# A decoder layer with routed experts on one core: zero rows by DMA, logits behind the first maxima, and a head group's last value products among the next group's first scores

## The chip, the core and the metric

The kernel runs on one core of a Trainium2 chip. TensorE (PE) multiplies matrices into PSUM, VectorE (DVE), ScalarE (ACT) and GpSimd (POOL) work on rows, and SyncE (SP) issues most of the DMAs. The metric is the time of one execution on the device in microseconds (us), the median of several runs.

## The reference, cut to what matters

```python
# x (4, 1024, 256), 16 heads of 16, rotary part of 32; cross attention over 77 keys; 8 experts, two for each token
x = layernorm(x + attention(x))        # causal, scores = (q.k + q_rope.k_rope) / sqrt(48), then W_o
x = layernorm(x + cross_attention(x, ctx, mask))   # softmax(q.k / 16) @ v, masked
probs = softmax(x @ Wr.T)              # the logits of the router
topw, topi = top_k(probs, 2); topw /= sum(topw)
y = sum over the two experts of gate * (silu(x @ w1[e]) * (x @ w3[e])) @ w2[e]
return layernorm(x + y)
```

## The kernel before, in words

Everything is in one program with a hand-written order on each engine and semaphores between them. After a start-up (constants, zeroed rows, projections of batch 0) it runs four batches, and after them the expert part over 72 blocks. Batch 0 and batch 3 are written out; batches 1 and 2 are one loop that runs twice.

**Attention of a batch** is done in four groups of four heads (`HG`). For each group there are two passes over scores. The first, `s1_unit` on PE (lines 754 and 758) and `maxima` on DVE (1271, 1274), only finds the row maxima; 24 units and one transposition (762) end in a 16 KB DMA of `nmaxT` into row 127 of `qs` (`MROW`, line 651). The second pass, `s2_unit` (777, 778), has the maximum folded in through that row, 12 steps of four heads, each followed on ACT by an exponential into `pT` (1142). On eight of the twelve steps, the diagonal ones, the last among them, POOL then zeroes later keys (`zero_later_keys`, 472). `pv_step` (792) multiplies with the values one step later (`LAG` = 1), and after the last step of a group ACT copies the result out of PSUM (`oT`, 1150). The units of the next group's first pass are strewn among this group's second pass by `due`, from `FIRST` and the tables of column counts; `ALONE_AT`, `COUNT_AT` and `PAIRED_AT` do this for group 0, in which the routing of the batch before also still runs.

**Operands.** `qs` and `kas` hold for two sets the rows 0 to 31 (parts of q or k), 32 to 95 (rotary parts) and 127; the rows 96 to 126 (`KROWS` to `MROW`, 31 rows) must be zero since the products run over 127 or 128 rows. `kbs` is the same for the low part of k. `kas` set 0 is used as other storage (`xTh`, `xTl`) for the projections of the next batch, and `kbs` for the cross attention, so their zero rows are written anew in each batch, by POOL: `zero_keys` (449) once the projections are through, and line 533 when the cross attention is through. Rows 96 to 126 of `qs` set 0 are zeroed once and stay zero.

**SP's order** (`first_groups`, 608, for the next batch): rotary rows of `qs` (592), `save_part` 0 to 5 (602), rotary rows of `kas`, the row of ones (606), `save_part` 6 and 7, a wait until all parts are in DRAM, loads of q and k of group 0 (570), then set 1, then, when the cross attention is through (642), the rotary rows of `kbs` and the low part of k (583). Later transfers on this queue, `nmaxT` too, stand behind these.

**Between two attentions** PE transposes `oT` (941), `att` (949), multiplies with W_o (732), transposes x for the cross attention (970), computes its scores (982), transposes its probabilities (992), multiplies with the values (999), transposes again (970) and computes the logits (1009, 32 products of 8 columns). `fill` puts the first maxima of the next batch's group 0 between these. On DVE `keep` and `neg` (1307, 1308) come first, then the chain of the normalizations (1335), and when all maxima are done `choose` (1413 on) does the routing; ACT gives it one exponential (1181), today before the exponentials of the next attention. POOL scatters the routed rows (`SENT`, 485) in groups 0 and 1 of the next attention.

Of the kernel before, what the change touches and what calls it, by code (L numbers as in the profile page):

```python
# [18 lines left out]
F32 = mybir.dt.float32  # L19
# [5 lines left out]
ACT = mybir.ActivationFunctionType  # L25
# [3 lines left out]
B, T, D = 4, 1024, 256  # L29
NT = T // P  # L30
# [4 lines left out]
NG = NH // HG  # L35
# [6 lines left out]
MROW = P - 1  # L42
# [37 lines left out]
LAG = 1  # L80
# [3 lines left out]
ALONE = SECOND  # L84
ALONE_AT = (0, 1, 3, 5, 7, 10, 12, 14)
AHEAD = 1
COUNT_AT, PAIRED_AT = 9, 15
LATE = (43, 39, 39, 39)
FIRST, SPARE = 1, 11
SENT = ((0, 0, 0, 2, 2, 2, 2, 2), (2, 2, 2, 0, 0, 0, 0, 0))  # L90

# [13 lines left out]
def layer(nc, x, ctxT, mask, w_all, kwT, qw, vwT, qb, kb, vb, wrT, w1, w3, w2, ident, causal, before,  # L105
          numbers, filling, rope, out):
    ctx = ExitStack()
    with ctx:
# [121 lines left out]
        with nc.Block() as block:  # L230
# [25 lines left out]
            @block.gpsimd  # L256
            def _(pool):
                pool.dma_start(xa[:, :, :], x[0].rearrange("(t p) d -> p t d", p=P)).then_inc(s_x, 16)

                pool.dma_start(xs[E * CAP:ROWS], filling[E * P:]).then_inc(s_sc, 16)  # L260
                pool.memset(wr[:, :, :], 0.0).then_inc(s_init, 1)
                pool.memset(m_all[:, :, :, :], 0.0).then_inc(s_init, 1)
                pool.memset(vall[:, :, :], 0.0).then_inc(s_init, 1)
                pool.memset(vaug[:, :, :, HD:HD + 1], 1.0).then_inc(s_init, 1)
                pool.memset(px[:, :, :], 0.0).then_inc(s_init, 1)
                pool.memset(one[:, :], 1.0).then_inc(s_init, 1)
                pool.memset(taken[:, :], 0.0).then_inc(s_init, 1)
                pool.memset(nhalf[:, :], -0.5).then_inc(s_init, 1)
                pool.wait_ge(s_init, 8)
                pool.memset(kbs[KROWS:MROW, :, :].bitcast(F32), 0.0).then_inc(s_zl, 1)  # L270
                pool.wait_ge(s_zl, 1)
                pool.memset(qs[KROWS:MROW, 0, :, :].bitcast(F32), 0.0).then_inc(s_zero, 1)
                pool.wait_ge(s_zero, 1)
                pool.memset(kas[KROWS:MROW, 1, :, :].bitcast(F32), 0.0).then_inc(s_zero, 1)
                pool.wait_ge(s_zero, 2)
# [144 lines left out]
        with nc.Block() as block:  # L420
            @block.gpsimd
            def _(pool):
# [19 lines left out]

                def zero_keys(b):

                    pool.wait_ge(s_pr, b * N_PROJ + QK[3] + 1)
                    pool.sem_inc(s_seen, 1)
                    pool.wait_ge(s_rs, b * 4 + 4)
                    pool.sem_inc(s_seen, 1)
                    pool.memset(kas[KROWS:MROW, 0, :, :].bitcast(F32), 0.0).then_inc(s_zk, 1)
                    pool.wait_ge(s_zk, b + 1)  # L450
                    pool.sem_inc(s_seen, 1)

                for m in range(4):
                    rope_add(0, m)
                    rope_low(0, m)
                zero_keys(0)
                for s in s_stg:
# [31 lines left out]
                def batch(b, then, ahead):  # L489
# [23 lines left out]

                    if then:
                        pool.wait_ge(s_tri, (b + 1) * NG * len(DIAG))
                        pool.sem_inc(s_seen, 1)
                        zero_keys(b + 1)
                    power(0, 0, s_ve1, s_pow1)
# [8 lines left out]
                    power(1, 1, s_ve2, s_pow2)  # L527
                    if then:
                        pool.wait_ge(s_t7, (b + 1) * NT)
                        pool.sem_inc(s_seen, 1)  # L530
                        pool.wait_ge(s_pow2, (b + 1) * 2)
                        pool.sem_inc(s_seen, 1)
                        pool.memset(kbs[KROWS:MROW, :, :].bitcast(F32), 0.0).then_inc(s_zl, 1)
                        pool.wait_ge(s_zl, b + 2)
                        pool.sem_inc(s_seen, 1)

# [27 lines left out]
            def _(sp):  # L564
# [43 lines left out]
                def first_groups(b, first):  # L608
# [8 lines left out]
                    place_rope(kas[:, 0], 2, s_qk[0])  # L617
                    place_ones(0)
                    for m in range(6, 8):
                        save_part(b, m)  # L620
# [19 lines left out]
                    if not first:  # L640
                        sp.wait_ge(s_t7, b * NT)
                        sp.sem_inc(s_spw, 1)
                    place_rope(kbs, 3, s_kb)
                    for h in range(2):
                        load_klow(b, 0, h)
# [82 lines left out]
            def _(pe):  # L728
# [119 lines left out]
                def first_maxima(b, n):  # L848

                    if n == 0:  # L850

                        pe.wait_ge(s_zk, b + 1)
                        if isinstance(b, int) and b == 0:
                            pe.wait_ge(s_zero, 1)
                        pe.wait_ge(s_vc, b * 4 + 4)
                        if not isinstance(b, int) or b > 0:
                            pe.wait_ge(s_t3r, b * NT)
                        heads_here(b, 0, 0)
                    if n == SECOND:
                        heads_here(b, 0, 1)  # L860
                    s1_unit(b, 0, n)
# [7 lines left out]
                def attention(b, then, ahead):  # L869
# [15 lines left out]
                    for g in range(NG):  # L885
                        done = 0
                        if g == 0:
                            pe.wait_ge(s_zl, b + 1)
                            heads_here(b, 1, 0)
# [7 lines left out]
                        for u in range(N_PV):  # L897
# [20 lines left out]
                            if u >= LAG:  # L918
                                pv_step(b, g, u - LAG)
                        for u in range(N_PV - LAG, N_PV):  # L920
                            pv_step(b, g, u)
                        assert g + 1 == NG or done == N_S1

                def batch(b, then, ahead):
# [78 lines left out]
                    turn(x2, s_ln2, s_t8, s_t8r)  # L1003
                    fill(12, 13, 14)
                    for hf in range(2):
# [5 lines left out]
                        ins.then_inc(s_t9, 1)  # L1011
                    fill(*range(15, N_S1))

# [91 lines left out]
            def _(act):  # L1105
# [25 lines left out]

                def batch(b, then):
                    for g in range(NG):
                        for u, (j, c) in enumerate(S2_STEPS):
# [4 lines left out]
                            for h in range(HG):  # L1139
                                n = g * N_S2 + u * HG + h  # L1140
                                act.wait_ge(s_s2, b * NG * N_S2 + n + 1)
                                act.activation(pT[:, u % 2, h, 0:q1 - q0], ps[:, s2_bank(n), q0 - w0:q1 - w0], ACT.Exp,  # L1142
                                               scale=ATT_SCALE).then_inc(s_exp, 1)
                            if then and g == NG - 1:
                                for m in LAST_ACT[u]:
                                    proj(b + 1, m)
                        act.wait_ge(s_pv, (b * NG + g + 1) * N_PV)
                        if g == 1:
                            act.wait_ge(s_left, b + 1)
                        act.activation(oT[:, g, :], ps[:, 6:8, :].rearrange("p c n -> p (c n)"), ACT.Copy).then_inc(s_oT, 1)  # L1150
                    for t in range(NT):
# [27 lines left out]
                    act.activation(x2b[:, :, 0:D], x2[:, :, 0:D], ACT.Copy).then_inc(s_x2b, 1)  # L1179
                    act.wait_ge(s_le, b + 1)  # L1180
                    act.activation(lg[:, 1, :, :], lg[:, 0, :, :], ACT.Exp).then_inc(s_lex, 1)

                for u in range(N_PROJ):
                    proj(0, u, True)
                batch(0, True)
                with act.Fori(1, B - 1) as b:
                    batch(b, True)
                batch(B - 1, False)

# [473 lines left out]
```

## Time and profile before

| | us |
|---|---|
| median of 3 runs | 1621.0 |
| lowest and highest | 1615.82 and 1627.38 |
| the profiled execution | 1616.89 |
| its span in the profile | 1615.2 |
| start-up, up to the first scores of batch 0 | 103.7 |
| PE busy | 1371.1 (85%) |
| DVE, ACT, POOL busy | 790.3, 624.1, 359.3 |

A profile gives for each engine the instructions with their start, and in brackets how long the engine was idle before one and what ended that idle time. The span is the time from the first to the last instruction.

### The profile page before, as it was taken

How to read it: one execution, taken by the hardware profiler on the slowest of the kernel's cores; microseconds unless marked ns; L12 is line 12 of the kernel's file. 1: busy time of each engine (PE TensorE's matmuls, PEld its weight loads, DVE VectorE, ACT ScalarE, POOL GpSimd, SP SyncE). 2: the span in 40 equal slices, each digit the busy share in tenths (PEclk: the TensorE clock that was granted, in tenths of full speed). 3: DMA queues.
4: the chain of work that ended last, by engine and by line, in shares of the span. 5: the costliest groups of instructions: out<-in, count | busy, mean ns of one | idle time of the engine just before them, and what ended most of it. 6: DMA issues, size and time to landing. Idle time of an engine off the chain costs nothing.

```text
span 1615.2 us, 25041 instructions
## 1 busy us (share of the span) xinstructions
PE 1371.1 (85%) x7580; PEld 959.9 (59%) x7581; DVE 790.3 (49%) x1636; ACT 624.1 (39%) x1327; POOL 359.3 (22%) x434
## 2 busy tenths in 40 slices
PE   3688999879899976989988799997359999999980
PEld 2545566655555564655566556555248888888870
DVE  3364452677544386644348655506733333333325
ACT  2124556313455521445642244562423333333324
POOL 5201112210411401131230132110332222222225
PEclk9789999968999996999988699998579999999995
DMA  4752113830321382032156212217311111111119
GB/s 148 205 97 41 29 20 100 199 63 1 87 47 42 118 171 41 12 83 40 43 165 123 40 46 47 40 42 260 105 56 53 49 49 52 52 49 49 52 38 310
DMA packets 87836, 131.80 MB, mean 82 GB/s; under 512 B 14944, under 2 KB 46944, under 8 KB 87584
## 3 DMA queue, kind: packets, MB, share of 16 engines
q1 hardware_dynamic: 74064, 100.98, 26.0%
q0 software_dynamic: 7936, 24.20, 4.6%
q10 hardware_dynamic: 5744, 5.43, 1.1%
q8 instruction: 53, 0.87, 0.2%
q14 instruction: 39, 0.32, 0.1%
HBM read 70.34 MB, written 40.98 MB: 69 GB/s over the span
## 4 chain that ended last, share of the span: by engine, by line
PE 70%; DVE 9%; issue 6%; DMA 6%; POOL 4%; ACT 2%; SPq 2%; ACTq 0%; POOLq 0%; DVEq 0%
PE ps L1089 13%; PE ps L777 11%; PE ps L754 10%; PE ps L778 8%; PE ps L1076 8%; PE ps L792 8%; DMA kas<-scr_k 3%; PE ps L732 3%; PE ps L758 2%; PE ps L1097 2%; DVE nmax L1274 2%; POOL xs L485 1%; PE ps L1059 1%; PE ps L1009 1%; DVE x L1335 1%
## 5 line engine op out<-in xcount | busy, mean ns | idle before, releaser
L1142 ACT ACTIVATE pT<-ps 128x512 f32<-128x512 f32 (+3 forms) x768 | 344.5, 493 | 349.0 <-PE ps L778 348.9
L1274 DVE TENSOR_REDUCE nmax<-ps 128x1 f32<-128x640 f32 (+3 forms) x256 | 258.5, 1024 | 118.6 <-PE ps L758 113.8
L777 PE MATMUL ps<-qs,kas 128*128 128x512 f32 (+2 forms) x768 | 308.7, 410 | 8.9 <-DMA qs<-nmaxT 5.3
L754 PE MATMUL ps<-kas,qs 127*128 127x512 f32 (+2 forms) x768 | 247.8, 412 | 27.1 <-DMA kas<-scr_k 16.2
L778 PE MATMUL ps<-qs,kbs 127*128 127x512 f32 (+2 forms) x768 | 268.0, 357 | 0.0
L777 PEld LDWEIGHTS ps<-qs,kas 128*128 128x128 f32 x768 | 150.2, 196 | 140.8 <-ACT pT L1142 102.2
L472 POOL TENSOR_SCALAR_AFFINE_SELECT pT<-pT 128x512 f32<-128x512 f32 x128 | 81.2, 634 | 661.9 <-ACT pT L1142 661.8
L754 PEld LDWEIGHTS ps<-kas,qs 127*128 127x128 f32 x768 | 152.0, 220 | 62.2 <-issue 12.9
L1271 DVE TENSOR_REDUCE nmax<-ps 128x2 f32<-128x256 f32 (+3 forms) x128 | 104.4, 825 | 151.0 <-PE ps L758 150.1
L792 PE MATMUL ps<-pT,vaug 128*17 128x512 f32 (+3 forms) x1536 | 161.2, 491 | 15.7 <-POOL pT L472 15.6
L778 PEld LDWEIGHTS ps<-qs,kbs 127*128 127x128 f32 x768 | 149.9, 195 | 5.4
L1076 PE MATMUL ps<-w2s,hidT 128*128 x576 | 136.1, 379 | 0.8 <-ACT hidT L1219 0.8
L1089 PE MATMUL ps<-w13h,xbh 128*128 x288 | 120.1, 417 | 0.1
L1076 PEld LDWEIGHTS ps<-w2s,hidT 128*128 128x128 f32 x576 | 109.1, 190 | 18.2 <-issue 1.0
L1219 ACT ACTIVATE hidT<-ps 128x512 f32<-128x512 f32 x72 | 43.0, 598 | 188.8 <-PE ps L1097 188.8
L1569 DVE TENSOR_TENSOR hid<-ps,sil 128x512 f32<-128x512 f32 x72 | 49.8, 692 | 134.1 <-PE ps L1089 134.1
L1089 PE MATMUL ps<-w13h,xbl 128*128 x288 | 114.6, 398 | 0.0
L1089 PE MATMUL ps<-w13l,xbh 128*128 x288 | 112.9, 392 | 0.0
L758 PE MATMUL ps<-cst_b 128*128 128x128 bf16 x512 | 105.8, 250 | 0.0
L758 PEld LDWEIGHTS ps<-cst_b 128*128 128x128 bf16 x512 | 44.2, 109 | 80.5 <-issue 75.9
L426 POOL TENSOR_TENSOR mark<-nhalf 128x1 f32<-128x1 f32 x76 | 14.0, 184 | 291.6 <-DVE yb L1579 271.8
L550 POOL DMA_INDIRECT sums<-yb,ib x72 | 70.8, 984 | 32.6 <-issue 32.3
(199 smaller groups left out, 1775.3 us busy)
## 6 DMA issues: line engine op xcount, KB each, us to landing
xb<-xs SPq DMA_DIRECT2D x72, 129.0 KB, 2.1
qs<-rs SPq DMA_DIRECT2D x32, 256.0 KB, 6.1
scr_q<-stg SPq DMA_DIRECT2D x16, 512.0 KB, 2.7
scr_k<-stg SPq DMA_DIRECT2D x16, 512.0 KB, 3.6
kas<-rs SPq DMA_DIRECT2D x32, 256.0 KB, 6.2
qs<-scr_q SPq DMA_DIRECT2D x64, 128.0 KB, 5.4
kas<-scr_k SPq DMA_DIRECT2D x64, 128.0 KB, 6.2
kbs<-scr_k SPq DMA_DIRECT2D x64, 128.0 KB, 4.1
```

The source lines that it names most:

```text
L472: pool.affine_select(pT[:, u % 2, :, 0:P], pT[:, u % 2, :, 0:P], pattern=[[0, HG], [1, P]], compare_op=ALU.is_ge, fill=zero, base=0, chann ...
L550: pool.indirect_dma_start(out=sums[:, :], out_offset=bass.IndirectOffsetOnAxis(ib[:, d, :], 0), in_=yb[:, d, :], in_offset=None).then_inc( ...
L754: ins = pe.matmul(ps[:, slot + bank, 0:n_k], qs[0:MROW, g % 2, h, i * P:(i + 1) * P], kas[0:MROW, g % 2, h, k0:k0 + n_k], start=True, stop ...
L758: ins = pe.matmul(ps[:, slot + own, i * P - k0:k1 - k0], idb, mask_q, start=False, stop=True)
L777: pe.matmul(o, kas[:, g % 2, h, j * P:(j + 1) * P], qs[:, g % 2, h, w0:q1], start=True, stop=False)
L778: pe.matmul(o, kbs[0:MROW, h, j * P:(j + 1) * P], qs[0:MROW, g % 2, h, w0:q1], start=False, stop=True).then_inc(s_s2, 1)
L792: ins = pe.matmul(ps[h * 32:h * 32 + HD + 1, 6 + c, q0 - c * HALF:HALF], vaug[:, j, g * HG + h, :], pT[:, u % 2, h, 0:q1 - q0], start=j == ...
L1076: ins = pe.matmul(ps[:, 7, 0:D], hidT[:, p, c, :], wide(w2s, e, c), start=c == 0, stop=c == F // P - 1)
L1089: ins = pe.matmul(ps[:, bank + p, :], a[:, p, c, :], wide(w, e, part, c), start=k == 0, stop=k == len(terms) - 1)
L1142: act.activation(pT[:, u % 2, h, 0:q1 - q0], ps[:, s2_bank(n), q0 - w0:q1 - w0], ACT.Exp, scale=ATT_SCALE).then_inc(s_exp, 1)
L1271: dve.tensor_reduce(nmax[:, k:k + NT + 1:NT], ps[:, slot:slot + 2, 0:(i + 1) * P], AX.X, ALU.max, negate=True).then_inc(s_s1r, 1)
L1274: dve.tensor_reduce(nmax[:, k:k + 1], ps[:, slot:slot + 2, :].rearrange("p s n -> p (s n)")[:, 0:(i + 1) * P], AX.X, ALU.max, negate=True) ...
```

## The change

Four things are done. The 31 zero rows of `kas` set 0 and of `kbs` come by a DMA on SP's queue from the rows of `qs` that stay zero, and POOL's memsets go, the one at the start too. The logits stand behind all first maxima, and their exponential on ACT behind the first four exponentials of the next attention. A group's last value products run behind the first four scores of the next group, with the copy of `oT` behind those four exponentials. The tables that place the units and POOL's scatters are set anew.

```diff
-ALONE_AT = (0, 1, 3, 5, 7, 10, 12, 14)
+ALONE_AT = (0, 5, 6, 8, 10, 13, 15, 17)
-COUNT_AT, PAIRED_AT = 9, 15
+COUNT_AT, PAIRED_AT = 12, 18
-FIRST, SPARE = 1, 11
-SENT = ((0, 0, 0, 2, 2, 2, 2, 2), (2, 2, 2, 0, 0, 0, 0, 0))
+FIRST, SPARE = 6, 11
+SENT = ((0, 0, 0, 4, 0, 0, 0, 0), (3, 3, 3, 3, 0, 0, 0, 0))
...
-                pool.memset(kbs[KROWS:MROW, :, :].bitcast(F32), 0.0).then_inc(s_zl, 1)
-                pool.wait_ge(s_zl, 1)
...
-                def zero_keys(b):
-
-                    pool.wait_ge(s_pr, b * N_PROJ + QK[3] + 1)
-                    pool.sem_inc(s_seen, 1)
-                    pool.wait_ge(s_rs, b * 4 + 4)
-                    pool.sem_inc(s_seen, 1)
-                    pool.memset(kas[KROWS:MROW, 0, :, :].bitcast(F32), 0.0).then_inc(s_zk, 1)
...
-                        pool.memset(kbs[KROWS:MROW, :, :].bitcast(F32), 0.0).then_inc(s_zl, 1)
...
                     place_rope(kas[:, 0], 2, s_qk[0])
                     place_ones(0)
+                    if first:
+                        sp.wait_ge(s_zero, 1)
+                    sp.dma_start(kas[KROWS:MROW, 0, :, :].bitcast(F32), qs[KROWS:MROW, 0, :, :].bitcast(F32)).then_inc(s_zk, 16)
                     for m in range(6, 8):
                         save_part(b, m)
...
                     place_rope(kbs, 3, s_kb)
+                    sp.dma_start(kbs[KROWS:MROW, :, :].bitcast(F32), qs[KROWS:MROW, 0, :, :].bitcast(F32)).then_inc(s_zl, 16)
                     for h in range(2):
                         load_klow(b, 0, h)
...
-                        pe.wait_ge(s_zk, b + 1)
+                        pe.wait_ge(s_zk, b * 16 + 16)
...
-                            pe.wait_ge(s_zl, b + 1)
+                            pe.wait_ge(s_zl, b * 16 + 16)
...
                             if u >= LAG:
                                 pv_step(b, g, u - LAG)
-                        for u in range(N_PV - LAG, N_PV):
-                            pv_step(b, g, u)
+                            elif g > 0:
+                                pv_step(b, g - 1, N_PV + u - LAG)
+                        if g + 1 == NG:
+                            for u in range(N_PV - LAG, N_PV):
+                                pv_step(b, g, u)
...
-                    fill(12, 13, 14)
+                    fill(*range(12, N_S1))
                     for hf in range(2):
                         pe.wait_ge(s_t8r, b * NT + 4 * hf + 4)
...
-                    fill(*range(15, N_S1))
...
+                def heads_out(b, g):
+                    act.wait_ge(s_pv, (b * NG + g + 1) * N_PV)
+                    if g == 1:
+                        act.wait_ge(s_left, b + 1)
+                    act.activation(oT[:, g, :], ps[:, 6:8, :].rearrange("p c n -> p (c n)"), ACT.Copy).then_inc(s_oT, 1)
+
+                def gates(b):
+                    act.wait_ge(s_le, b + 1)
+                    act.activation(lg[:, 1, :, :], lg[:, 0, :, :], ACT.Exp).then_inc(s_lex, 1)
...
+                            if ahead and g == 0 and u == 0:
+                                gates(b - 1)
+                            if g > 0 and u == LAG - 1:
+                                heads_out(b, g - 1)
...
-                    act.wait_ge(s_le, b + 1)
-                    act.activation(lg[:, 1, :, :], lg[:, 0, :, :], ACT.Exp).then_inc(s_lex, 1)
```

## Rows read from the trace of the kernel before

**Rows 1.** Windows view: PE, PEld, DVE, ACT, POOL busy, clock, DMA share, GB/s
```profile
292.00:376.00 84.00, 65.23 (x330) 47.30 (x331) 65.91 (x147) 16.20 (x35) 11.87 (x7) 0.73 0.52 108
```
**Rows 2.** Timeline of POOL and DVE around the memset of kas, batch 0
```profile
291.84 3.51 POOL L449 MEMSET kas<- 31x4096 f32 x1 [0.15 <-POOL rs L440]
...
292.00 3.69 DVE L1307 TENSOR_SCALAR keep<-mk 128x616 f32<-128x616 uint8 x1
295.60 0.46 DVE L1308 TENSOR_SCALAR neg<-mk 128x616 f32<-128x616 uint8 x1
```
**Rows 3.** Timeline of PE behind it
```profile
296.87 0.69 PE L949 MATMUL ps<-idf,att 128*128 128x128 f32 x2 [3.39 <-DVE att L1343]
```
**Rows 4.** Timeline of DVE and POOL around the memset of kbs, batch 0
```profile
341.82 1.35 DVE L1335 TENSOR_SCALAR x<-x,mv,rstd 128x256 f32<-128x256 f32 x4
...
345.78 4.74 DVE L1335 TENSOR_SCALAR x<-x,mv,rstd 128x256 f32<-128x256 f32 x4 [0.39 <-POOL rstd L512]
...
345.90 3.51 POOL L533 MEMSET kbs<- 31x4096 f32 x1 [0.15 <-POOL rstd L512]
```
**Rows 5.** Timeline of PE and DVE, logits to second pass, batches 0 to 1
```profile
354.69 3.86 PE L1009 MATMUL ps<-wr,x2T 128*128 128x8 f32 x32
...
359.56 2.08 DVE L1274 TENSOR_REDUCE nmax<-ps 128x1 f32<-128x768 f32 x2 [3.71 <-PE ps L758]
...
370.86 0.37 PE L762 MATMUL ps<-idf,nmax 128*32 128x128 f32 x1 [1.41 <-DVE nmax L1274]
...
373.94 0.79 PE L777 MATMUL ps<-qs,kas 128*128 128x512 f32 x1 [1.70 <-DMA qs<-nmaxT]
```
**Rows 6.** Timeline of PE, the same place between batches 1 and 2
```profile
646.76 0.79 PE L754 MATMUL ps<-kas,qs 127*128 127x256 f32 x2 [4.91 <-issue]
```
**Rows 7.** Timeline of PE, group ends in batches 0 and 1
```profile
198.70 0.41 PE L792 MATMUL ps<-pT,vaug 128*17 128x128 f32 x8 [0.61 <-POOL pT L472]
201.52 0.51 PE L754 MATMUL ps<-kas,qs 127*128 127x256 f32 x2 [1.26 <-DMA kas<-scr_k]
421.04 0.41 PE L792 MATMUL ps<-pT,vaug 128*17 128x128 f32 x8 [2.39 <-POOL pT L472]
424.33 0.80 PE L754 MATMUL ps<-kas,qs 127*128 127x256 f32 x2 [1.68 <-DMA kas<-scr_k]
```
**Rows 8.** Windows view, what the 16 DMA engines move together
```profile
45.00:47.00 2.00, 0.49 (x3) 0.05 (x1) 0.00 (x0) 0.39 (x1) 2.00 (x1) 1.00 1.05 405
...
293.50:296.00 2.50, 0.00 (x0) 0.00 (x0) 2.50 (x2) 0.00 (x0) 1.84 (x1) 0.50 0.94 201
...
95.00:101.00 6.00, 3.37 (x14) 1.70 (x14) 5.74 (x6) 0.00 (x0) 0.00 (x0) 1.00 0.94 178
```
**Rows 9.** Timeline of SP and PE, start-up
```profile
60.69 1.70 SPq L602 DMA_DIRECT2D scr_k<-stg  x2
65.82 0.82 SPq L570 DMA_DIRECT2D qs<-scr_q  x2
...
86.83 3.64 SPq L592 DMA_DIRECT2D kbs<-rs  x4
...
74.84 0.76 PE L754 MATMUL ps<-kas,qs 127*128 127x256 f32 x2 [3.31 <-DMA kas<-scr_k]
...
103.68 0.80 PE L777 MATMUL ps<-qs,kas 128*128 128x512 f32 x1 [2.07 <-DMA qs<-nmaxT]
```
**Rows 10.** Timeline of SP and PE, loads of batch 1 before its first maxima
```profile
296.26 1.68 SPq L602 DMA_DIRECT2D scr_k<-stg  x2
301.55 0.81 SPq L570 DMA_DIRECT2D qs<-scr_q  x2
...
318.17 0.47 PE L754 MATMUL ps<-kas,qs 127*128 127x256 f32 x2
```
**Rows 11.** Timeline of SP, rows of kbs for batch 2
```profile
612.22 3.18 SPq L592 DMA_DIRECT2D kbs<-rs  x4
615.50 3.37 SPq L583 DMA_DIRECT2D kbs<-scr_k  x4
```

More of the change, by code:

```diff
@@ L441, in rope_low @@
                                        ALU.subtract).then_inc(s_rs, 1)
-                def zero_keys(b):
-                    pool.wait_ge(s_pr, b * N_PROJ + QK[3] + 1)
-                    pool.sem_inc(s_seen, 1)
-                    pool.wait_ge(s_rs, b * 4 + 4)
-                    pool.sem_inc(s_seen, 1)
-                    pool.memset(kas[KROWS:MROW, 0, :, :].bitcast(F32), 0.0).then_inc(s_zk, 1)
-                    pool.wait_ge(s_zk, b + 1)
-                    pool.sem_inc(s_seen, 1)
                 for m in range(4):
@@ L455, in _ @@
                     rope_low(0, m)
-                zero_keys(0)
                 for s in s_stg:
@@ L512, in power @@
                         pool.tensor_tensor(rstd[:, k, half], ve[:, k, half], nhalf[:, half], ALU.pow).then_inc(done_sem, 1)
[L514 to L517, printed above, removed]
                     power(0, 0, s_ve1, s_pow1)
@@ L527, in batch @@
                     power(1, 1, s_ve2, s_pow2)
[L528 to L532, printed above, removed]
-                        pool.memset(kbs[KROWS:MROW, :, :].bitcast(F32), 0.0).then_inc(s_zl, 1)
-                        pool.wait_ge(s_zl, b + 2)
-                        pool.sem_inc(s_seen, 1)
                 batch(0, True, False)
@@ L1130, in proj, with batch @@
                                        proj_bank(u, first).rearrange("p (t h d) -> p t h d", t=2, h=NH), ACT.Copy).then_inc(s_vc, 1)
-                def batch(b, then):
+                def heads_out(b, g):
[6 more added lines that the diff above has]
+                    act.activation(lg[:, 1, :, :], lg[:, 0, :, :], ACT.Exp).then_inc(s_lex, 1)
+                def batch(b, then, ahead):
                     for g in range(NG):
@@ L1146, in batch @@
                                     proj(b + 1, m)
[L1147 to L1150, printed above, removed]
+                    heads_out(b, NG - 1)
                     for t in range(NT):
@@ L1179, in batch @@
                     act.activation(x2b[:, :, 0:D], x2[:, :, 0:D], ACT.Copy).then_inc(s_x2b, 1)
-                    act.wait_ge(s_le, b + 1)
-                    act.activation(lg[:, 1, :, :], lg[:, 0, :, :], ACT.Exp).then_inc(s_lex, 1)
                 for u in range(N_PROJ):
                     proj(0, u, True)
-                batch(0, True)
+                batch(0, True, False)
                 with act.Fori(1, B - 1) as b:
-                    batch(b, True)
-                batch(B - 1, False)
+                    batch(b, True, True)
+                batch(B - 1, False, True)
+                gates(B - 1)
                 act.wait_ge(s_x, (B + 1) * 16)
```

## Prediction

> **What bounds the kernel now.** I read the windows view by stage first. Within the four head groups PE is nearly always busy, so only its own gaps count there. Between two attentions it is not: of 84 us PE works 65, at a mean clock of 0.73 of full speed, and DVE works 66 [rows 1]. There the timelines of DVE, POOL and PE, laid side by side, show which instruction the next one waits for. Last I read SP's timeline, since two transfers are put into it.
>
> **POOL's memsets, removed.** Each clears 31 rows of 4096 values in 3.51 us, and each stands exactly over a DVE instruction that grows by that much. `keep` takes 3.69 us under the memset of `kas`, while its twin `neg`, of the same size, takes 0.46 [rows 2]; the four normalizations take 4.74 under the memset of `kbs`, and 1.35 in the first half of the same batch [rows 4]. PE stands behind both: it waits 3.39 us for the first `att` [rows 3], and it needs the normalized rows for the next transpositions. In the loop the same pattern repeats, three times in all. `keep` would give 3.2 us, of which I count 2.7, since the transpositions end only about 1 us after `keep` starts. The normalization gives 4.74 - 1.35 = 3.4. Gain: 3 x (2.7 + 3.4) = 18 us.
>
> **Logits moved.** Today they hold PE for 3.86 us amid the first maxima, and DVE starves for 3.71 us [rows 5]. That gap goes. Behind the last transposition (370.86 + 0.37) the second pass now starts 2.7 us later, at 373.94, covered by the DMA of `nmaxT`. After the change the logits (3.9) and one unit (1.0) stand there: 4.9 us, 2.2 more, and the DMA is hidden under them. Net gain 1.5 us. At the turn of the loop (batch 1 to 2) PE idles 4.91 us anyway [rows 6], so nothing is covered there and the move is worth 0. Gain: 2 x 1.5 = 3 us. The clock is at 1.2 GHz around this place (0.43 us for 512 columns); that the logits keep PE busy up to the second pass could raise it earlier. I count nothing for it.
>
> **The gates' exponential.** It now waits for the first four exponentials, some 3 us, and DVE's routing, on which the next group's maxima hang, with it. `ALONE_AT` gives the units of that time later places. PE then has scores alone, paced by ACT, and catches up later. Bounds 0 and 3 us a batch; I take 1.5. Loss: 3 x 1.5 = 4.5 us.
>
> **Group ends.** Today PE waits 0.61 us for POOL's select, then 1.26 for the next but one group's k [rows 7]. After: scores 0 to 3 run at ACT's pace on two PSUM banks (about 0.4 idle), and score 6 waits for the copy of `oT`, about 1 us that now stands between exponentials 3 and 4. That is 1.4 against 1.9. At the end of group 0 in batches 1 to 3 the select is late by 2.39 since scatters are issued before it, and k costs 1.68 [rows 7]; `SENT` clears the select, but the low part of k for the next group then becomes the later one, so I count 0.5 there too. Bounds -1 and +2 for each of the 12 ends; sum: 8 x 0.4 = 3 us gain (group 2 to 3, where projections fill the time, 0).
>
> Together these give 18 + 3 - 4.5 + 3 = 19.5 us of gain.
>
> **The zero rows as a DMA.** This is the dear part. Each transfer is 31 rows x 16 KB = 508 KB. No row of before shows a transfer of 31 rows; all its row counts are multiples of 16, the number of engines that share a transfer. Ends: shared evenly it takes 508 KB / 405 GB/s = 1.3 us. But 31 rows can't be dealt out in equal whole rows to 16 engines, nor to any number of them but one; on one engine, at a sixteenth of 405 GB/s (25.3), it takes 20.1 us, and at a sixteenth of the 201 GB/s of the copies of rotary rows, 12.6, it takes 40 [rows 8]. I take one engine and 20 us: the slow copies have all 16 engines at the same 32 rows, one engine alone has not.
>
> The Trainium skill ("DMA: Bandwidth & Descriptors", section on why a DMA increments its semaphore by 16) says that a DMA from SP runs on the largest number of engines up to 16 that divides the slowest dimension of both sides, and names 127 partitions as a case of one engine; by that rule 31 rows are such a case. It speaks against this change; no run here shows it yet.
>
> What stands behind such a transfer? Every later transfer on SP's queue has a sixteenth of its bytes on that engine, behind those 20 us.
>
> *Start-up.* The zero rows of `kas` stand ahead of the last two saves (60.69), whose landing at 65.8 releases the loads, and PE starts the maxima on the loads at 74.84 [rows 9]. Plus 20. From there SP's list up to the end of the rotary rows of `kbs` (86.83 + 3.64) takes 24.6 us, 2 of them a wait that falls away: 85.8 + 22.6 = 108.4. The queues are then some 7 us behind, as they are now (0.94 busy up to 101, SP's last issue at 94.6) [rows 8], so the zero rows of `kbs` move from 115.5 to 135.5, then the low part of k and `nmaxT`: 138.5. The second pass would have been ready at 103.7 + 20 = 123.7. Plus 15. Start-up: 35 us lost.
>
> *Batches 0, 1, 2, `kas`.* The zero rows wait for the rotary rows until 297.7, last to 317.7, and the saves land 20 us later: the loads start at 321.6 instead of 301.55. In the start-up loads needed 9.0 us until PE could run [rows 9], here I take 6.5 (fewer transfers beside them): 328. PE wants them at 318.17 - 2.7 = 315.5 [rows 10]. 12.5 us late, three times, 37.5 us. After such a halt PE restarts at 1.2 GHz, where this stretch ran at 2.4 today: about 1.5 us each, 4.5 us.
>
> *`kbs`.* The rotary rows start at 612.2 [rows 11] and end at about 618, the zero rows at 638, the low part of k and `nmaxT` at 641. PE is ready at 641.8 - 3.4 - 4 + 4 of logits + 4.9 of the turn + 1 = 644 in the loop: hidden. Between batches 0 and 1, and 2 and 3, there is no turn: 2 us late each, 4 us.
>
> Cost: 35 + 37.5 + 4.5 + 4 = 81 us. Sum against the profiled execution: 1617 - 19.5 + 81 = 1678. Its own time, 1616.89, lies 4 us below the median and within the three runs, so I leave the number at 1678.
>
> **Rivals.** (a) *The 31 rows are spread over the engines.* Each transfer then costs some 1 us of issue and 1.3 of queue, hidden in the batches (PE comes 16 us after the loads start [rows 10]), 2 us in the start-up: 1617 - 19.5 + 2 = 1600, faster. For it: the copies of 32 rows are spread. Against: they divide by 16. Decides from: a transfer of under some 8 us leaves all batches covered. (b) *One engine, but later transfers don't queue behind it.* Then only the waits for the zeroes themselves count: start-up 8 for `kas` (82 against 74.8) and about 8 for `kbs`, 3 a batch at `kas`: 25 - 19.5: 1622, no change. Against: the copies of rotary rows do hold up what is behind them, the low part of k in the start-up. (c) *One engine at 12.6 GB/s.* 20 us more in eight places (two in the start-up, three and three in the batches): 1678 + 160 = 1838. Against: the rows at 201 GB/s have a common port of 32 rows as the likelier limit.
>
> **Chances.** Forecast (one engine, about 20 us) 0.80; (a) 0.12; (b) 0.04; (c) 0.04. Within the forecast the transfer may take 19 to 29 us (up to not quite halfway to the slow end; 7 to 8 us of total for each us of it), and my covers may be off by some 4 us in each of the eight places: 1635 to 1750. The range is that of the forecast, which leaves out (a) and (c). Within 1% is about what a measurement of this kernel can tell from no change, and here is 1605 to 1637. Faster by over 1%: 0.11; within 1%: 0.06; slower: 0.83.
>
> **What would show it.** The transfer's time from issue to landing in the DMA section: about 20 us or about 4. `keep` at about 0.5 us and all normalizations at 1.35 per four, in every case. PE waiting for `kas` or `qs` before the first unit of each batch, 20 us in the start-up and about 12 in the batches; the second pass of batch 0 starting near 138. A first pass without DVE's gap of 3.7. If the transfers land in 3 to 4 us, the forecast is wrong in sign, and (a) holds.

## The result and the profile after

| | before | after |
|---|---|---|
| median on the same chip, 4 runs each, us | 1624.2 | 1697.3 |
| lowest and highest | 1615.8, 1633.1 | 1694.4, 1699.5 |
| ratio, 95% interval | | 1.044 (1.040 to 1.048) |
| span of the profiled execution | 1615.2 | 1692.5 |

The change makes the kernel 4.4% slower. In the profiled executions 77.3 us are lost. The table says where. A stage begins or ends with the start of the first or last instruction of a kind on PE: first maxima are line 754 of before and 733 of after, the second pass is line 777 and 756.

| stage, us | before | after | difference |
|---|---|---|---|
| start to the second pass of batch 0 | 103.7 | 142.4 | +38.7 |
| four attentions (second passes) | 720.1 | 726.6 | +6.5 |
| end of an attention to the first maxima, three times | 30.0, 30.9, 31.8 | 42.9, 44.3, 42.7 | +37.0 |
| first maxima to the second pass, three times | 55.8, 58.8, 56.4 | 56.1, 55.5, 55.2 | -3.9 |
| the rest (end of batch 3 and experts) | 527.7 | 526.7 | -1.0 |

Page of the kernel after: SP's queue and the DMA issues (the last column is us from issue to landing).

```profile
q1 hardware_dynamic: 74320, 105.04, 25.7%
...
scr_q<-stg SPq DMA_DIRECT2D x16, 512.0 KB, 2.7
scr_k<-stg SPq DMA_DIRECT2D x16, 512.0 KB, 14.2
```

`scr_k<-stg` are the saves, half of which stand behind the zero rows; their median was 3.6 us before and is 14.2 now, while the saves of q, ahead of the zero rows, still take 2.7. The queue had 74064 packets before and has 256 more: 32 for each of the eight zero transfers, that is 31 rows of 16 KB and a single closing packet. One closing packet means one engine, as the cut transfers below show. This is what the DMA view says of 13 us in the middle of the first zero transfer:

```profile
GB/s 50 0 50 0 50 0 50 0 50 0 50 50 0 50 0 50 0 50 0 50 0 50 0 50 0 50 50 0 50 0 50 0 50 0 50 0 50 0 50 0
DMA packets 21, 0.34 MB, mean 26 GB/s; under 512 B 0, under 2 KB 0, under 8 KB 0
```

21 packets in 13 us: one after the other, about 0.62 us each, 26 GB/s, and nothing else moves. The recorded estimate was 25.3. Timelines of SP and PE in the start-up, after:

```profile
60.77 1.31 SPq L596 DMA_DIRECT2D kas<-qs  x1
62.22 1.78 SPq L577 DMA_DIRECT2D scr_k<-stg  x2
87.19 0.82 SPq L545 DMA_DIRECT2D qs<-scr_q  x2
103.89 0.66 SPq L622 DMA_DIRECT2D kbs<-qs  x1
...
96.35 0.77 PE L733 MATMUL ps<-kas,qs 127*128 127x256 f32 x2 [24.25 <-DMA kas<-scr_k]
141.06 0.77 PE L733 MATMUL ps<-kas,qs 127*128 127x256 f32 x2 [18.41 <-DMA kbs<-qs]
142.44 0.80 PE L756 MATMUL ps<-qs,kas 128*128 128x512 f32 x1 [0.38 <-DMA qs<-nmaxT]
```

The loads (line 545) start 25 us after the saves and not 5 [rows 9], so PE has its first operands at 96.35 instead of 74.84. Then the zero rows of `kbs` hold it once more, for 18.4 us. The same, once, before batch 1:

```profile
335.54 1.14 SPq L596 DMA_DIRECT2D kas<-qs  x1
336.80 0.92 SPq L577 DMA_DIRECT2D scr_k<-stg  x2
361.60 0.81 SPq L545 DMA_DIRECT2D qs<-scr_q  x2
...
370.35 0.77 PE L733 MATMUL ps<-kas,qs 127*128 127x256 f32 x2 [16.17 <-DMA kas<-scr_k]
```

In the chain that ended last, the pieces for the same transfer are the longest of all:

```profile
62.74 24.38 DMA scr_k<-stg
122.98 19.41 DMA qs<-nmaxT
337.31 24.22 DMA scr_k<-stg
625.29 23.85 DMA scr_k<-stg
909.55 23.88 DMA scr_k<-stg
```

The memsets' cost has gone as forecast. DVE of after, `keep` and the two halves of the second normalization:

```profile
331.35 0.47 DVE L1297 TENSOR_SCALAR keep<-mk 128x616 f32<-128x616 uint8 x1
396.78 1.35 DVE L1325 TENSOR_SCALAR x<-x,mv,rstd 128x256 f32<-128x256 f32 x4
400.73 1.38 DVE L1325 TENSOR_SCALAR x<-x,mv,rstd 128x256 f32<-128x256 f32 x4 [0.39 <-POOL rstd L499]
```

0.47 was 3.69 [rows 2], and 1.38 was 4.74 [rows 4].

Last, the logits. PE of after, and windows of before and of after around them (columns as in rows 1; the third number from the right is the granted clock):

```profile
417.09 0.37 PE L741 MATMUL ps<-idf,nmax 128*32 128x128 f32 x1 [1.55 <-DVE nmax L1264]
417.26 6.84 PE L991 MATMUL ps<-wr,x2T 128*128 128x8 f32 x32
425.05 0.79 PE L733 MATMUL ps<-kas,qs 127*128 127x256 f32 x2 [0.96 <-DMA kbs<-qs]
```

Before:

```profile
354.69:358.55 3.86, 3.86 (x35) 3.86 (x35) 0.96 (x1) 0.00 (x0) 0.00 (x0) 0.94 0.02 4
360.00:371.00 11.00, 9.46 (x25) 4.79 (x23) 9.79 (x9) 0.00 (x0) 0.00 (x0) 0.50 0.00 0
```

After:

```profile
406.00:417.00 11.00, 7.40 (x30) 3.83 (x28) 10.59 (x11) 0.00 (x0) 0.00 (x0) 0.96 0.09 33
417.26:424.10 6.84, 6.84 (x33) 6.74 (x32) 0.28 (x1) 0.00 (x0) 0.00 (x0) 0.50 0.07 29
```

The same 32 products take 6.84 us instead of 3.86. Before they ran at 0.94 of the clock (the 2.4 GHz level), and the maxima behind them at 0.50 (1.2 GHz). Now it is the other way round: the last maxima, in which PE waits for DVE (busy 10.59 of 11.00), have the high clock, and it falls just as the logits begin. The maxima gain by it. These are the twelfth and the ninth pair of maxima ahead of the transposition (370.86 before [rows 5], 417.09 after), before and then after:

```profile
351.61 0.99 PE L754 MATMUL ps<-kas,qs 127*128 127x512 f32 x2
358.40 0.99 PE L754 MATMUL ps<-kas,qs 127*128 127x512 f32 x2
```

```profile
403.19 0.99 PE L733 MATMUL ps<-kas,qs 127*128 127x512 f32 x2
406.27 0.85 PE L733 MATMUL ps<-kas,qs 127*128 127x512 f32 x2
```

The last nine take 12.5 us up to the transposition before and 10.8 after; all twelve, with the logits among them before, 19.3 and 13.9. Behind the transposition the second pass comes after 3.1 us before and after 9.4 now, of which 0.96 is the wait for `kbs`.

That the new place has brought the low clock is not shown. The five kernels below that leave the logits where they were (ends_only, zero_dma_only, zero_two_only, zero_30_1, zero_on_pool) run them three times each between two attentions, and in 10 of these 15 places they took 6.94 us as well (3.8 to 4.6 in the others); in the seven kernels below that move them they took 6.83 or 6.84 in 14 of 21 places (4.8 to 5.3 in the others). In ends_only, in the old place:

```profile
355.55 6.94 PE L1012 MATMUL ps<-wr,x2T 128*128 128x8 f32 x32
```

So which of two neighbouring stretches had the high clock changed from kernel to kernel at either place, and the profile of before, with 3.8 to 4.4 us in all three, is the one in which the logits were quick each time.

The clock behind PE's halt for `kas` is a third stretch. Windows from the first maxima on, before and then after:

```profile
318.17:324.00 5.83, 5.73 (x51) 5.06 (x50) 3.44 (x6) 0.39 (x2) 0.00 (x0) 1.00 1.06 260
```

```profile
370.35:376.00 5.65, 5.65 (x28) 5.26 (x29) 2.24 (x4) 0.00 (x0) 0.00 (x0) 0.50 1.05 165
```

1.00 of the clock before and 0.50 after the halt; the first six pairs of maxima and the two sets of scores among them take 9.0 us instead of 6.6.

### The profile page after: what moved, and what is told of

Its sections match the earlier page's. It is cut to its first block, busy times and chain, and to the rows that moved or that the text cites. A ratio compares the mean times of both kernels' runs of the same rounds, so it can differ in the third digit from the quotient of the medians.

```text
span 1692.5 us, 25005 instructions
## 1 busy us (share of the span) xinstructions
PE 1381.4 (82%) x7580; PEld 957.3 (57%) x7581; DVE 768.3 (45%) x1636; ACT 623.8 (37%) x1327; POOL 331.1 (20%) x426
## 4 chain that ended last, share of the span: by engine, by line
PE 64%; DMA 13%; DVE 10%; issue 3%; ACT 3%; POOL 3%; SPq 2%; ACTq 0%; DVEq 0%; POOLq 0%
PE ps L1070 12%; PE ps L756 11%; PE ps L733 8%; PE ps L771 8%; PE ps L757 8%; PE ps L1057 7%; DMA scr_k<-stg 6%; DMA qs<-nmaxT 3%; PE ps L711 3%; DVE nmax L1264 3%; PE ps L1078 2%; PE ps L737 2%; DMA kas<-scr_k 2%; DVE nmax L1261 2%; DMA kbs<-scr_k 1%
## 5 line engine op out<-in xcount | busy, mean ns | idle before, releaser
L733 PE MATMUL ps<-kas,qs 127*128 127x512 f32 (+2 forms) x768 | 235.8, 394 | 114.0 <-DMA kas<-scr_k 69.9
L733 PEld LDWEIGHTS ps<-kas,qs 127*128 127x128 f32 x768 | 139.9, 206 | 147.1 <-issue 61.6
L1261 DVE TENSOR_REDUCE nmax<-ps 128x2 f32<-128x256 f32 (+3 forms) x128 | 103.5, 823 | 237.5 <-PE ps L737 235.5
L737 PE MATMUL ps<-cst_b 128*128 128x128 bf16 x512 | 102.0, 242 | 0.0
## 6 DMA issues: line engine op xcount, KB each, us to landing
scr_k<-stg SPq DMA_DIRECT2D x16, 512.0 KB, 14.2
```

The source lines that it names most:

```text
L733: ins = pe.matmul(ps[:, slot + bank, 0:n_k], qs[0:MROW, g % 2, h, i * P:(i + 1) * P], kas[0:MROW, g % 2, h, k0:k0 + n_k], start=True, stop ...
L737: ins = pe.matmul(ps[:, slot + own, i * P - k0:k1 - k0], idb, mask_q, start=False, stop=True)
L1261: dve.tensor_reduce(nmax[:, k:k + NT + 1:NT], ps[:, slot:slot + 2, 0:(i + 1) * P], AX.X, ALU.max, negate=True).then_inc(s_s1r, 1)
```

## Experiments

Ratios are to the kernel before on the same chip; its median varied from 1625.9 to 1633.1 between chips, so kernels of different rows are compared by their ratio. Each kernel computes the whole result.

| kernel | median us | ratio (95%) | start to second pass |
|---|---|---|---|
| zero_dma_only | 1701.4 | 1.043 (1.039 to 1.047) | 143.1 |
| zero_two_only | 1614.1 | 0.988 (0.984 to 0.992) | 113.2 |
| zero_30_1 | 1610.4 | 0.990 (0.986 to 0.993) | 105.8 |
| zero_on_pool | 1606.2 | 0.986 (0.983 to 0.989) | 105.5 |
| after_memset | 1620.8 | 0.995 (0.992 to 0.998) | 103.5 |
| logits_only | 1625.8 | 1.000 (0.997 to 1.002) | 103.7 |
| logits_early_exp | 1620.6 | 0.997 (0.994 to 0.999) | 105.7 |
| ends_only | 1622.2 | 0.997 (0.995 to 1.000) | 104.0 |
| after_two | 1607.4 | 0.985 (0.981 to 0.988) | 111.6 |
| after_two_late | 1599.5 | 0.983 (0.980 to 0.986) | 103.8 |
| after_30_late | 1600.8 | 0.984 (0.982 to 0.987) | 103.7 |
| best_early_exp | 1601.1 | 0.984 (0.981 to 0.987) | 104.9 |

### Is the loss in the zero rows?

**zero_dma_only** is the kernel before with the zero rows by the change's DMAs and nothing else.

```diff
-                    pool.memset(kas[KROWS:MROW, 0, :, :].bitcast(F32), 0.0).then_inc(s_zk, 1)
-                        pool.memset(kbs[KROWS:MROW, :, :].bitcast(F32), 0.0).then_inc(s_zl, 1)
+                    sp.dma_start(kas[KROWS:MROW, 0, :, :].bitcast(F32), qs[KROWS:MROW, 0, :, :].bitcast(F32)).then_inc(s_zk, 16)
+                    sp.dma_start(kbs[KROWS:MROW, :, :].bitcast(F32), qs[KROWS:MROW, 0, :, :].bitcast(F32)).then_inc(s_zl, 16)
```

> The kernel before with one part of the change: the two memsets of POOL are gone, and the 31 zero rows come by one DMA each on SP's queue, ahead of the saves (kas) and behind the rotary rows (kbs). Logits, gates, group ends and SENT are as before. Theory A (one engine carries the whole transfer, all that follows on SP's queue waits for it): the loss of the change is all here. The trace of after puts 38.7 us in the start-up and 12.3 us per batch (three times) in front of the first maxima, together 76; of the other parts I take at most 3 us either way. Expected 1624 + 73 to 1624 + 80 = 1697 to 1704 us, saves landing after 24 us. Theory B (the transfers cost only their own wait, and the logits, the gates' exponential or the group ends cost the rest): 1624 - 18 + 25 = about 1631.

Measured 1.043, against 1.044 for the whole change. **after_memset** is the other half, the kernel after with the memsets in place of the DMAs:

> The kernel after with the memsets of POOL back in place of the two DMAs: what is left is the logits behind the first maxima, the gates' exponential behind the first four exponentials, the group ends and SENT. Theory A with the sizes of the recorded sum (3 gained on the logits, 4.5 lost on the exponential, 3 gained on group ends): 1624 - 1.5 = 1622 us. From the trace of after, where the four attentions are 6.5 us longer and the stretches from first maxima to second pass 3.9 us shorter: 1624 + 3 = 1627. Theory B (these parts carry the loss): over 1660.

Measured 0.995 (0.992 to 0.998), a small gain of about 8 us where 3 lost to 1.5 gained were expected. So the zero transfers carry the whole loss. In its trace DVE still pays for the memset, and PE behind it, which ties the cost of rows 2 and 3 to the memset alone:

```profile
291.12 3.70 DVE L1318 TENSOR_SCALAR keep<-mk 128x616 f32<-128x616 uint8 x1
...
296.00 0.69 PE L952 MATMUL ps<-idf,att 128*128 128x128 f32 x2 [3.47 <-DVE att L1354]
```

### Is it the bytes, the place, or the number of rows?

**zero_two_only** leaves bytes and place and cuts each transfer in two.

```diff
-                    sp.dma_start(kas[KROWS:MROW, 0, :, :].bitcast(F32), qs[KROWS:MROW, 0, :, :].bitcast(F32)).then_inc(s_zk, 16)
+                    for r0, r1_ in ((KROWS, KROWS + 16), (KROWS + 16, MROW)):
+                        sp.dma_start(kas[r0:r1_, 0, :, :].bitcast(F32), qs[r0:r1_, 0, :, :].bitcast(F32)).then_inc(s_zk, 16)
```

> As the kernel with the zero rows alone by DMA, but each transfer of 31 rows is cut into two, of 16 and of 15 rows; the bytes and the places in the queue are the same, one more issue each. Theory A (the number of rows decides on how many engines a transfer runs; 16 rows on 16, 15 rows on 15 or 5 or 3): each takes 2 to 3 us, nothing stands behind it, the memsets' 18 us stay as gain: 1624 - 18 + 2 to + 6 = 1608 to 1612 us; were the 15 rows also on one engine, 10 us each, some 1650. Theory C (it is the bytes of 508 KB or the place ahead of the saves, whatever the engines): no better than the single transfer, 1690 or more.

> The kernel before with the zero rows by DMA, each transfer of 31 rows cut into one of 30 rows and one of 1 row. It tells the size of a transfer from the number of its rows: the first has 97% of the bytes of the single transfer. If it is the number of rows (the largest divisor up to 16: 30 rows on 15 engines, 1 row on one for under 1 us), it is as good as the cut into 16 and 15, ratio 0.988, 1611 to 1618 us, and the packets of SP's queue are again 31 + 16 at each of eight places (74064 + 376 = 74440). If only numbers that 16 divides are spread, or the bytes decide, it is about as slow as the single transfer, 1690 to 1700.

Both cuts turn the loss of 4.3% into a gain of 1.0 to 1.2%, some 87 us (1701.4 to 1614.1, the same chip) for one more issue in eight places. Pages of zero_two_only:

```profile
q1 hardware_dynamic: 74560, 105.04, 28.3%
...
scr_k<-stg SPq DMA_DIRECT2D x16, 512.0 KB, 6.1
```

of zero_30_1:

```profile
q1 hardware_dynamic: 74680, 105.04, 27.3%
...
scr_k<-stg SPq DMA_DIRECT2D x16, 512.0 KB, 3.5
```

The packets tell the engines. With 16 and 15 rows there are 496 more than before, 62 for each place: 31 rows and 31 closing packets, 16 engines and 15. So 15 rows do run on 15 engines, and it isn't multiples of 16 that are spread. With 30 and 1 there are 616, 77 for each: 30 rows with 15 closing ones make 45, and the other 32 are a single row cut into 16 pieces, with 16 closing packets: the trace has 240 packets of 16 KB (8 x 30) and, in the eight places, 128 more of 1 KB than before (8 x 16). I had expected 376, as the single row was taken to stay on one engine; that part of the expectation was wrong, and it costs nothing. A transfer with 97% of the bytes of the slow one is no slower than the halves, so it is the number of rows.

By the rule of the Trainium skill ("DMA: Bandwidth & Descriptors", section on why a DMA increments its semaphore by 16) 31 rows give 1 engine, 30 gives 15, 16 gives 16 and 15 gives 15; the packets agree with all four.

The cuts aren't alike in the start-up. SP of zero_two_only and then of zero_30_1:

```profile
63.03 4.19 SPq L577 DMA_DIRECT2D scr_k<-stg  x2
71.47 0.82 SPq L545 DMA_DIRECT2D qs<-scr_q  x2
```

```profile
62.65 2.41 SPq L577 DMA_DIRECT2D scr_k<-stg  x2
68.53 0.82 SPq L545 DMA_DIRECT2D qs<-scr_q  x2
```

With 16 and 15 the loads come 8.4 us after the saves, with 30 and 1 5.9, with the memset 5.1 [rows 9]. Why one way of cutting is dearer where the bytes are the same wasn't tried.

**zero_on_pool** keeps the single transfer of 31 rows but issues it from POOL, where the memsets stood.

```diff
-                    pool.memset(kas[KROWS:MROW, 0, :, :].bitcast(F32), 0.0).then_inc(s_zk, 1)
-                    pool.wait_ge(s_zk, b + 1)
-                    pool.sem_inc(s_seen, 1)
+                    pool.dma_start(kas[KROWS:MROW, 0, :, :].bitcast(F32), qs[KROWS:MROW, 0, :, :].bitcast(F32)).then_inc(s_zk, 16)
```

> The kernel before with the single transfers of 31 rows, but issued by POOL where its memsets stood, on POOL's queue and not on SP's. It tells whether later transfers wait because they are behind it on the same queue, or because its one engine is busy for 19 us (31 packets of 611 ns) for every queue. Queue: SP's saves and loads are not held up, so only PE's own waits for the zeroes count: some 8 us in the start-up and 1 to 3 in each batch against the 18 us of the memsets: about 1610 to 1620 us, saves landing after 4 to 6 us. Engine: a save needs all 16 engines, so it waits as before: saves landing after some 13 us or more, about 1680 to 1700 us. In between, if the engine takes packets of both queues in turn: the saves' share of that engine takes about twice as long, 1615 to 1630.

It came out at 0.986, under all three expectations, since they all took the one engine for granted. DMA view of the stretch 297 to 312 us, POOL's queue and its transfer:

```profile
q0 software_dynamic: 48, 0.51, 16.1%
...
scr_k<-stg SPq DMA_DIRECT2D x2, 512.0 KB, 5.7
kas<-qs POOLq DMA_DIRECT2D x1, 496.0 KB, 5.9
```

The same 31 rows land in 5.9 us, beside other transfers, where SP's took over 20 (in the start-up of after, issued at 60.77, its last packet ends at 84.2). 48 packets are 31 rows and 17 more, where one engine would leave 32. The transfer is spread when POOL issues it. So the question it was made for, whether one busy engine also holds up the other queue, stays open: there was no busy engine. The Trainium skill ("DMA: Bandwidth & Descriptors", section on why a DMA increments its semaphore by 16) states this case: some direct copies issued by GpSimd get all 16 engines even where the number of partitions has no divisor; the trace agrees.

### What the other parts are worth

**logits_only** moves the logits and the gates' exponential; **logits_early_exp** moves the logits and leaves the exponential. Both have the new `ALONE_AT`, `COUNT_AT` and `PAIRED_AT`.

```diff
-                    fill(12, 13, 14)
+                    fill(*range(12, N_S1))
...
-                    fill(*range(15, N_S1))
```

> The kernel before with the logits behind the last first maxima, the gates' exponential behind the first four exponentials and the later places of what waits for it; zero rows, group ends and SENT as before. The recorded sum: 2 x 1.5 gained, 3 x 1.5 lost: ratio 1.001. From the traces (first maxima to second pass: 55.8, 58.8, 56.3 before; 56.2, 55.5, 55.3 after; 51 to 54 where the transfers are spread and the memsets gone): gained by 0 to 12 us in all, ratio 0.993 to 1.000; the upper end only if the gap of DVE is what counts and the late exponential costs nothing.

> The kernel before with the logits behind the last first maxima, but the gates' exponential in its old place on ACT, ahead of the next batch's exponentials. Against logits_only (ratio 0.9998) it gives the price of the late exponential. The recorded sum has it at 1.5 us a batch: ratio 0.997. Rival: in its old place ACT waits for the logits, for their copy and for the maxima on DVE before it may do the first exponential of the attention, while PE stands before two full banks of scores: 2 to 3 us lost a batch, ratio 1.003 to 1.005.

1.000 and 0.997, with intervals that overlap: a cost of 0.3%, 5 us, for the late exponential is the best estimate, with an uncertainty as large. The traces show how it acts. DVE and PE of logits_only:

```profile
377.92 0.22 DVE L1423 TENSOR_REDUCE sl<-lg 128x8 f32<-128x64 f32 x1 [4.62 <-ACT lg L1133]
...
379.75 0.50 PE L754 MATMUL ps<-kas,qs 127*128 127x256 f32 x2 [0.88 <-DVE nmax L1274]
```

DVE of logits_early_exp:

```profile
379.61 0.22 DVE L1419 TENSOR_REDUCE sl<-lg 128x8 f32<-128x64 f32 x1 [0.32 <-ACT lg L1180]
```

With the late exponential the routing waits 4.62 us and PE 0.88; with the early one the routing waits 0.32, and the timeline shows no wait of PE up to 392 us. The rival, that ACT would be blocked by the early one, didn't come true. But in the best kernel, where the same edit was made (**best_early_exp**), it brought nothing, 0.984 against 0.983, so that the late exponential costs anything is not shown:

> after_two_late with the gates' exponential in its old place at the end of a batch on ACT. Between the two kernels with the logits moved the early exponential was the faster by 0.3% (0.9966 against 0.9998, intervals that overlap). If that adds up: 0.983 - 0.003 = 0.980 to the kernel before. If in the whole change nothing hangs on it: 0.983 or more.

**ends_only** has the group ends, `FIRST` and `SENT`:

```diff
                             if u >= LAG:
                                 pv_step(b, g, u - LAG)
-                        for u in range(N_PV - LAG, N_PV):
-                            pv_step(b, g, u)
+                            elif g > 0:
+                                pv_step(b, g - 1, N_PV + u - LAG)
```

> The kernel before with a group's last value products among the next group's first scores, the copy of oT behind the first four exponentials, FIRST 6 and the new SENT; zero rows and logits as before. The recorded sum: 8 x 0.4 = 3 us gained, ratio 0.998, bounds -1 and +2 for each of 12 ends: 0.985 to 1.007. In the traces of after the four attentions together are 3.7 to 6.5 us longer: ratio 1.002 to 1.004 if that is due to this part.

0.997 (0.995 to 1.000). PE at the end of group 0 of batch 1:

```profile
424.74 0.50 PE L777 MATMUL ps<-qs,kas 128*128 128x512 f32 x1 [1.66 <-DMA kbs<-scr_k]
426.16 0.50 PE L777 MATMUL ps<-qs,kas 128*128 128x512 f32 x1 [0.23 <-ACT pT L1151]
429.47 0.50 PE L777 MATMUL ps<-qs,kas 128*128 128x512 f32 x1 [0.63 <-ACT pT L1151]
```

The waits are 2.5 us where they were 4.1 [rows 7]: the select is covered, and the low part of k is now the late one, as forecast.

### The change with its transfers put right

**after_two** is the whole change with transfers of 16 and 15 rows. **after_two_late** gives the start-up its memsets back and puts the batches' zero rows of `kas` behind the last saves; **after_30_late** is the same with 30 and 1.

```diff
                     for m in range(6, 8):
                         save_part(b, m)
+                    if not first:
+                        for r0, r1_ in ((KROWS, KROWS + 16), (KROWS + 16, MROW)):
+                            sp.dma_start(kas[r0:r1_, 0, :, :].bitcast(F32), qs[r0:r1_, 0, :, :].bitcast(F32)).then_inc(s_zk, 16)
```

> The whole change, with each transfer of 31 rows cut into one of 16 and one of 15 rows. Theory A: the sum of the kernel with the cut transfers alone (1608 to 1612) and of the rest (-2 to +3): 1606 to 1615 us. By the recorded rival of evenly spread rows it would be 1600. If cutting doesn't help, about 1697 as the changed kernel.

> The whole change with transfers of 16 and 15 rows, but in the start-up the zero rows come by POOL's memsets as in the kernel before (one behind the others at the very start, one behind the rotary rows), and in the batches the two transfers for kas stand behind the last two saves, not ahead of them. In the trace with 16 and 15 rows the start-up up to the second pass is 8.1 us longer than before, and SP waits 9.0 us from the issue of the last saves to the loads, where it was 5. If those are the memsets' cover that was given up and the place in the queue: 8 us less in the start-up, and 0 to 2 a batch: ratio to the kernel before about 0.9845 - 0.006 = 0.979 (0.976 to 0.981), some 9 to 12 us under the plain cut. If the start-up needs its 8 us for other reasons: 0.984.

> The whole change with the start-up's zero rows by POOL's memsets and the batches' behind the saves, as in after_two_late, but cut into 30 rows and 1 row. With 30 and 1 the saves landed after 3.5 us (16 and 15: 6.1), and the loads followed 5 us after them (16 and 15: 9). In after_two_late the zero rows no longer stand ahead of the saves (3.7 us), so nothing should be left to gain: ratio 0.983 again, 0.980 to 0.985.

0.985, 0.983 and 0.984. Medians aside (they are from different chips), the intervals overlap, so these can't be ranked; each is faster than before by more than 1%. The start-up did give its 8 us back (111.6 to 103.8 us in the profiles, like before), but the ratio fell by 0.0015, not by the 0.006 expected. Each ratio is known to about 0.003, so the runs can't tell what those 8 us are worth in the whole. SP of after_two_late before batch 1:

```profile
296.81 1.67 SPq L590 DMA_DIRECT2D scr_k<-stg  x2
298.52 2.93 SPq L611 DMA_DIRECT2D kas<-qs  x2
303.17 1.91 SPq L558 DMA_DIRECT2D qs<-scr_q  x2
```

The saves are no longer behind anything, and the zero rows go out while SP waits for them. Against before, this profile has the three stretches from the end of an attention to the first maxima at 26.1, 27.9 and 28.0 us (30.0 to 31.8 before), the three behind them at 50.6, 54.0 and 49.1 (55.8 to 58.8).

## Why the prediction was right, and where its terms were off

1678 us were forecast, in a range of 1635 to 1750, slower; measured were 1697. The mechanism and its rivals fell as they should: the spread rows of rival (a) need another cut or another queue; (b) is refuted by the saves that land after 24 us; (c) by packets of 0.62 us, 26 GB/s. The stages of the forecast's sum, beside what they measured:

| | forecast | measured |
|---|---|---|
| start-up | +35 | +38.7 |
| to the first maxima: `kas` rows 37.5, less `keep` 8 | +29.5 | +37.0 |
| first maxima to second pass: clock 4.5, `kbs` rows 4, less normalizations 10 and logits 3 | -4.5 | -3.9 |
| attentions: gates 4.5, less group ends 3 | +1.5 | +6.5 |
| rest | 0 | -1.0 |
| sum | 61.5 | 77.3 |

- **One engine, 20 us.** Right. The packets take 31 x 0.62 = 19 us; with the wait for the engine, the saves behind them land 24 us after their issue, 25 in the forecast's batches. One reading behind it was too quick: not all row counts of before are multiples of 16 on both sides, since row 127 is written alone, from 32 rows (`kas<-one`, 16 KB). Nothing in the sum hung on it.
- **Start-up.** 21.5 us for `kas` (20 forecast) and 17.2 for `kbs` (15). The first steps were right in place and within 2 us in size.
- **`kas` in the batches.** The loads started 24.8 us behind the saves, as forecast; from there PE needed 8.8 us (361.60 to 370.35), and 8.3 and 8.4 in the next two batches, of which I had counted 6.5. This is the step that was short: 2 us in each batch. The start-up's row said 9.0 [rows 9], and I had cut it with no row for it. The table has this stage 7.5 us over the forecast, nearly half of the 16 by which the sum was short; this step makes up 6 of those 7.5.
- **Clock behind the halt.** Right in kind, and too small where it was read: 9.0 us instead of 6.6 before batch 1, 2.4 for the 1.5 forecast.
- **Memsets.** Right: 3.2 and 3.4 us each are gone from DVE.
- **Logits.** This term was wrong in its working. The forecast said that the new place has the clock at 1.2 GHz, and still put 3.9 us there, a time that was measured at 0.94 of the clock, near 2.4 GHz. There the logits took 6.84 us, 3.0 more. The other half was missing too: the nine maxima before the transposition ran faster, 10.8 us for 12.5. Before batch 1 the stretch of these maxima became 5.4 us shorter where 3.7 were forecast, and what stands behind the transposition 5.4 longer, without the wait for `kbs`, where 2.2 were forecast: net 0, not 1.5 gained. So two errors nearly cancel, and that the whole stage came within 0.6 us of the forecast is luck in part. logits_only, with the exponential in it, agrees as far as it can: 1.000. That the move itself changed the clock is not shown, as said above.
- **Gates.** The mechanism is in the trace (4.62 us of waiting on DVE, 0.88 on PE). The 1.5 us a batch fit the 0.3% between the two kernels, but neither these nor best_early_exp show that the cost differs from 0.
- **Group ends.** 0.997, about 5 us gained where 3 were forecast; right in sign, with an interval that reaches almost to 1. The waits at the end of group 0 fell by 1.6 us, where 0.5 was counted.
- **`kbs` in the batches.** 2 us were forecast where there is no turn of the loop; before batch 1 PE waited 0.96 for these rows behind the logits, which were 3.0 us longer than in the forecast.
- **The four attentions** are 6.5 us longer in the profile of after, where 1.5 were forecast: 5 us of the 16. They are 3.6 us longer in after_memset, 12 in logits_only and 7 in logits_early_exp, and 3.5 shorter in ends_only. But they are also 3.3 us longer in zero_two_only, 4.7 in zero_dma_only and 6.0 and 6.3 in zero_on_pool and zero_30_1, which change nothing in the attentions themselves. So nothing shows that the moved logits or the routing's later places cost these 5 us; the profile of before may just be a quick one. It stays open.
- **The sum.** By the profiles it was short by 16 us: 7.5 at `kas`, 5 in the attentions, 3.7 in the start-up, 0.6 behind the first maxima, less 1.0 in the rest. The profile of before lies at the low end of its runs, though: by the ratios 3.8% was forecast (61.5 of 1617) and 4.4% (4.0 to 4.8) measured, which is 10 us more than the forecast. The halves, zero_dma_only and after_memset, give 1.043 x 0.995 = 1.038, with an uncertainty of about 0.005, so nothing shows that they act on each other.

## What to carry to other kernels

Before a memset is turned into a DMA, factor its number of rows. 31 rows on SP's queue went through one engine at 26 GB/s and held up all behind them; the same rows as 16 and 15, as 30 and 1, or issued by POOL, cost next to nothing, and doing without the memsets was then worth 1.0 to 1.4%. Look in the packet count for the number of closing packets: it is the number of engines (for POOL's queue here it was 17, one more than 16). And when a piece of work bound by PE is moved, look up the clock at both places before its time is carried along: here 3.86 us near 2.4 GHz were put where the forecast itself had 1.2 GHz, and they became 6.84. Look also at what the other stretch gains, and at more than one profile: in these kernels the same products took between 3.8 and 6.9 us in one and the same place.

## What was not expected of the hardware

- The same transfer of 31 rows was spread when POOL issued it (48 packets, 5.9 us to landing) and was not when SP did (32 packets, over 20 us).
- A transfer of a single row of 16 KB from SP came as 16 pieces with 16 closing packets: 77 packets for each pair of 30 rows and 1 row, among them 16 of 1 KB.
- The clock was at 0.96 over a stretch in which PE worked 7.40 of 11.00 us, and fell to 0.50 at its end, where it stayed while PE was busy for all of the next 6.84 us.
